# A recommendation tower on one core: the scaled fields go to SBUF, PSUM banks are handed out one at a time, and each tile's sum is taken in two longer reduces

## The reference

```python
e = stack([tbl_f[ids[:, f]] for f in range(39)], axis=1)      # [1024, 39, 16]
x0 = xk = e
for W in (f0, f1, f2):                                        # [39*39,128], [128*39,128], [128*39,128]
    z = einsum('bfd,bgd->bfgd', x0, xk).reshape(b, f * g, d)
    cur = einsum('bpd,pm->bmd', z, W); outs.append(cur); xk = cur
z = sum(concatenate(outs, axis=1), axis=-1)                   # [1024, 384]
h = relu(concat([z, dense_ctx]) @ W_top1 + b_top1)
h = relu(h @ W_top2 + b_top2)
y = h @ W_top3                                                # [1024, 1]
```

## Time and profile before

| | |
|---|---|
| median of 3 runs | 1430.03 us (1429.89 to 1432.74) |
| profiled execution | 1431.03 us, its span 1429.3 us |
| mean granted TensorE clock | 0.987 of full speed |
| PE busy | 1308.0 us (92%) |
| DVE busy | 1128.8 us (79%) |
| ACT busy | 931.4 us (65%) |
| POOL busy | 661.0 us (46%) |

### The profile page before, as it was taken

The page is one execution under the profiler, slowest core; times in us unless marked ns, Lnnn a source line. Parts: engine busy times, 40 slices in busy tenths (PEclk is TensorE's granted clock), DMA queues, the critical chain, the costliest instruction groups (busy, mean ns, idle before and its releaser), DMA issues.

```text
span 1429.3 us, 21569 instructions
## 1 busy us (share of the span) xinstructions
PE 1308.0 (92%) x6680; PEld 984.6 (69%) x6680; DVE 1128.8 (79%) x2797; ACT 931.4 (65%) x3235; POOL 661.0 (46%) x634
## 2 busy tenths in 40 slices
PE   0399999999999999999999999999999999999998
PEld 0356666767777776777777677777767777776777
DVE  2168888888888888788878888788887888787884
ACT  1147776676666677667767667666766677676664
POOL 7785446554444556444455544445464432222100
PEclk9999999999999999999999999999999999999999
DMA  5171021100311012110211003110121002110000
GB/s 134 37 215 40 13 68 49 48 27 3 97 32 35 26 34 76 41 30 13 68 48 48 26 3 93 29 41 27 26 84 42 29 13 66 46 46 25 1 1 1
DMA packets 51178, 63.60 MB, mean 45 GB/s; under 512 B 13067, under 2 KB 24344, under 8 KB 51019
## 3 DMA queue, kind: packets, MB, share of 16 engines
q1 hardware_dynamic: 34544, 56.08, 12.8%
q0 software_dynamic: 10128, 2.98, 1.9%
q10 hardware_dynamic: 6392, 3.18, 0.9%
HBM read 11.08 MB, written 1.02 MB: 8 GB/s over the span
## 4 chain that ended last, share of the span: by engine, by line
PE 65%; DVE 16%; ACT 10%; issue 5%; POOL 3%; DMA 1%; ACTq 0%; DVEq 0%
PE Y L849 14%; PE Y L851 13%; PE Y L850 13%; PE C L783 13%; ACT Y L543 9%; PE C L806 5%; DVE sum_b L694 4%; POOL rows L398 3%; DVE sum_a L694 3%; DVE sum_a L699 3%; DVE part L694 2%; PE C L799 2%; DVE z L663 1%; PE C L824 1%; DVE Y L716 1%
## 5 line engine op out<-in xcount | busy, mean ns | idle before, releaser
L543 ACT ACTIVATE Y<-Y,x_col 128x128 f32<-128x128 f32 x2944 | 792.9, 361 | 387.7 <-PE Y L851 387.1
L849 PE MATMUL Y<-f_high,cur_high 128*128 128x512 f32 (+1 forms) x1280 | 614.5, 480 | 13.3 <-DVE part L707 9.1
L850 PE MATMUL Y<-f_low,cur_high 128*128 128x512 f32 (+1 forms) x1280 | 501.8, 392 | 0.0
L851 PE MATMUL Y<-f_high,cur_low 128*128 128x512 f32 (+1 forms) x1280 | 501.5, 392 | 0.0
L434 POOL TENSOR_TENSOR pairs<-shifted,base 117x512 f32<-117x512 f32 x186 | 240.6, 1295 | 524.1 <-PE C L783 522.4
L398 POOL DMA_INDIRECT rows<-in_tbl_dram,ids_sb x312 | 306.9, 984 | 77.4 <-issue 65.8
L849 PEld LDWEIGHTS Y<-f_high,cur_high 128*128 128x128 f32 x1280 | 243.5, 190 | 124.2 <-issue 54.9
L850 PEld LDWEIGHTS Y<-f_low,cur_high 128*128 128x128 f32 x1280 | 244.4, 191 | 87.3 <-issue 54.3
L851 PEld LDWEIGHTS Y<-f_high,cur_low 128*128 128x128 f32 x1280 | 242.5, 189 | 51.6
L694 DVE SCALAR_TENSOR_TENSOR sum_b<-Y,x_col,sum_b 128x128 f32<-128x128 f32 x768 | 262.7, 342 | 0.2 <-DVE part L694 0.2
L783 PE MATMUL C<-pairs,f_sum 117*128 117x512 f32 (+1 forms) x448 | 241.6, 623 | 5.7 <-DVE pairs L657 5.7
(11 more groups left out here) (92 smaller groups left out, 823.2 us busy)
## 6 DMA issues: line engine op xcount, KB each, us to landing
shifted<-x_seq SPq DMA_DIRECT2D x157, 234.0 KB
base<-x_seq SPq DMA_DIRECT2D x95, 78.0 KB
rows<-in_tbl_dram,ids_sb POOLq DMA_INDIRECT x312
shifted<-x_seq SPq DMA_DIRECT2D x31, 156.0 KB
G<-in_L_rec_f_dram ACTq DMA_DIRECT2D x3, 832.0 KB, 11.8
w_sb<-in_W_top_dram SPq DMA_DIRECT2D x1, 768.0 KB, 13.5
f_ext<-in_L_rec_f_dram SPq DMA_DIRECT2D x1, 760.5 KB
w_sb<-in_W_top_dram SPq DMA_DIRECT2D x1, 512.0 KB, 5.7
```

The costliest lines, as they stand in the source:

```text
L543: ins = act.activation(where[:, i * M:(i + 1) * M], where[:, i * M:(i + 1) * M], ACT.Copy, scale=x_col[:, t // JT % QG, t % JT, f:f + 1])
L849: pe.matmul(where, ch, wh, start=True, stop=False)
L850: pe.matmul(where, ch, wl, start=False, stop=False)
L851: pe.matmul(where, cl, wh, start=False, stop=True).then_inc(y_filled, 1)
```

## The change

ScalarE no longer scales in place: it writes the scaled blocks to a new SBUF tile `scaled_x` of 27 blocks of 128 values. The chunks it takes are now 0, 2, 4, 5, 7 and 8 (24 blocks), and VectorE's fused ones are 1, 3, 6 and 9 (15 blocks). Blocks 0 to 11 of `scaled_x` are chunks 0, 2 and 4; block 12 is the sum of these, block 13 and 14 are the two running sums, and blocks 15 to 26 are chunks 5, 7 and 8. VectorE takes two reduces in a tile, both out of SBUF with neighbouring values 512 bytes apart: one over blocks 0 to 11 (12 x 128 values) into block 12, and one over blocks 12 to 26 (15 x 128 values) into `cur1`. The two additions and the third reduce are gone. `scaled_x` exists once, so ScalarE's chunk 0 of a tile waits for the first reduce of the tile before and its chunk 5 for the second.

The six banks are given out one at a time. A bank is free as soon as ScalarE has scaled its chunk or the fused instructions have read it (`bank_free`). The `G` products take two single banks.

```diff
-UNITS = CH // 2
-UB = 3
-SCALED_UNITS = (0, 2, 4)
-SCALED = tuple(c for c in range(CH) if c // 2 in SCALED_UNITS)
+BANKS = 6
+FUSED = (1, 3, 6, 9)
+SCALED = tuple(c for c in range(CH) if c not in FUSED)
 NSC = len(SCALED)
-SUM_SLOT = 3
-R0, FUSE2, FUSE3, R1, FUSE6, FUSE7, JOIN, MERGE, R2 = 1, 2, 6, 10, 11, 15, 19, 20, 21
-NST = 21
-FREED = {0: R0, 1: R0, 2: FUSE2 + 3, 3: FUSE3 + 3, 4: R1, 5: R1, 6: FUSE6 + 3, 7: MERGE, 8: R2, 9: R2}
+HALF = 4 * (NSC // 2)
+FIRST_SUM, SUM_A = HALF, HALF + 1
+PLACE = {c: 4 * i + (3 if i >= NSC // 2 else 0) for i, c in enumerate(SCALED)}
+PLACES = 4 * NSC + 3
+FUSE = {1: 1, 3: 5, 6: 9, 9: 14}
+R0, R1 = 13, 17
+NST = 17
...
-        sum_a = sb("sum_a", [P, 2, M])
-        sum_b = sb("sum_b", [P, 2, M])
-        part = sb("part", [P, 2, M])
+        scaled_x = sb("scaled_x", [P, PLACES, M])
...
             def scale_chunk(t, c):
                 act.wait_ge(y_filled, CH * t + c + 1)
+                if t and c in (SCALED[0], SCALED[NSC // 2]):
+                    act.wait_ge(acc_steps, NST * (t - 1) + (R0 if c == SCALED[0] else R1))
                 where = bank(t, c)
                 for i, f in enumerate(CH_F[c]):
-                    ins = act.activation(where[:, i * M:(i + 1) * M], where[:, i * M:(i + 1) * M], ACT.Copy,
+                    ins = act.activation(scaled_x[:, PLACE[c] + i, :], where[:, i * M:(i + 1) * M], ACT.Copy,
                                          scale=x_col[:, t // JT % QG, t % JT, f:f + 1])
                 ins.then_inc(scaled, 1)
...
             def tile(t, g, q, j):
                 n0 = NST * t
-                dve.wait_ge(scaled, NSC * t + 2)
-                dve.tensor_reduce(sum_a[:, t % 2, :], unit(t, 0), AX.X, ALU.add).then_inc(acc_steps, 1)
-                fuse(t, 2, FUSE2, 0)
-                fuse(t, 3, FUSE3, 0)
+                fuse(t, FUSED[0])
+                fuse(t, FUSED[1])
                 if j == 0 and q and g >= QG:
                     layer2_read(g // QG - 1, q - 1)
                 if j == JT - 1 and g + 1 < NG:
                     split_cur0(g + 1)
-                dve.wait_ge(scaled, NSC * t + 4)
-                dve.tensor_reduce(part[:, t % 2, :], unit(t, 2), AX.X, ALU.add).then_inc(acc_steps, 1)
-                fuse(t, 6, FUSE6, 1)
-                fuse(t, 7, FUSE7, 1)
...
+                fuse(t, FUSED[2])
+                dve.wait_ge(scaled, NSC * t + NSC // 2)
+                dve.tensor_reduce(scaled_x[:, FIRST_SUM, :], scaled_x[:, 0:HALF, :].rearrange("p s m -> p m s"),
+                                  AX.X, ALU.add).then_inc(acc_steps, 1)
+                fuse(t, FUSED[3])
+                dve.wait_ge(scaled, NSC * t + NSC)
+                dve.wait_ge(acc_steps, n0 + R1 - 1)
                 if j == 0 and g >= 2:
                     dve.wait_ge(s_filled, S_USE["G", g - 2] + 1)
-                dve.tensor_reduce(cur1[:, t % CUR1_RING, :], unit(t, 4), AX.X, ALU.add).then_inc(acc_steps, 1)
+                dve.tensor_reduce(cur1[:, t % CUR1_RING, :], scaled_x[:, FIRST_SUM:PLACES, :].rearrange("p s m -> p m s"),
+                                  AX.X, ALU.add).then_inc(acc_steps, 1)
...
+            def bank_free(use):
+                previous = BANK_PREVIOUS.get(use)
+                if previous and previous[0] == "G":
+                    _, n, r = previous
+                    pe.wait_ge(g_read, 2 * n + r - 1)
+                elif previous:
+                    _, t, c = previous
+                    if c in FUSED:
+                        pe.wait_ge(acc_steps, NST * t + FUSE[c] + len(CH_F[c]) - 1)
+                    else:
+                        pe.wait_ge(scaled, NSC * t + SCALED.index(c) + 1)
```

## The result

The changed kernel takes 1559.93 us (median of 4 runs, 1558.06 to 1560.57), against 1429.96 for the kernel before in the same comparison: a ratio of 1.0915, 95% interval 1.0874 to 1.0955. The forecast was 1559 us. Its profiled execution took 1559.51 us, the span is 1557.8 us.

A forecast was written before the change was run, and what follows sets the result against it. VectorE was to replace TensorE as the bound, its SBUF reduces costing 1.81 ns a value: 84.0 + 44.2 + 1368 (thirty groups at 45.6) + 44.4 + 18.5 = 1559 us, 9% above now. The range was 1450 to 1685 us.

The forecast's parts named there:

- VectorE becomes the bound: Per group: VectorE would need 44.2 us where the kernel takes 41.5, replacing TensorE as the bound.
- 1.81 ns a value: SBUF reduces: rate for values 512 bytes apart, taken from line 636's copy of 624 values, against 1.04 in PSUM.
- The lower bound of 1.63: SBUF reduces: ns a value if a fixed part of 212 ns holds for line 636; total 1493 us, 1450 without stall.
- rival 2: SBUF reduces at half rate by VectorE's own clock, 2.08 ns a value, reduces 3.26 and 4.06 us; 1674 us, chance 0.17.
- A tile at 10.7 us: VectorE's work a tile: fused instructions 3.9, first reduce 2.85, second 3.55, waits for results 0.40 us.
- The stall of 1.4 us in tile 1: VectorE waits for chunk 6 in 31 groups, while TensorE does chunk 5, a first-layer sum and chunk 6 after chunk 1's bank frees.
- The total: Whole kernel: 84.0, group 0 at 44.2, thirty groups at 45.6, the last at 44.4, 16.8 and 1.7; 1559 us.
- Rival 1: SBUF reduces at full rate, 1.04 ns a value, TensorE stays the bound and banks free earlier; 1378 us, chance 0.19.
- about 43 us at the `G` products and 10 at the chunks: TensorE's waits for VectorE that the banks' earlier release would remove if the reduces ran at full rate.
- The turning point: Reduce rate at which VectorE's group, stall included, is 41.5 us, as the kernel now takes: about 1.5 ns a value.
- Rival 3: SBUF reduces wait for GpSimd, 0.3 us each, 256 of them 77 us on top of the forecast; 1636 us, chance 0.05.
- The new waits of ScalarE: Chunks 0 and 5 wait for VectorE's reduces, leaving ScalarE half a tile ahead of need; `C` wanted at slot 13 only.

The follow-up runs named there:

- e1: Changed kernel with both reduces reading neighbouring values of the same SBUF blocks instead of values 512 bytes apart; 1351.64 us, ratio 0.9428 to the kernel before.
- e5: Changed kernel with one first-layer sum of each group moved from ahead of chunk 6 of tile 1 to ahead of chunk 7; 1532.95 us, ratio 1.0711.
- e2: Changed kernel with only the first reduce (line 697) reading neighbouring values; 1448.78 us, ratio 1.0094 to the kernel before.
- e3: Changed kernel whose reduces read by turns in twelve patterns of steps and neighbours, each on its own line; first reduce 1745 ns or 2881 to 3078 ns.
- e4: Changed kernel with 28 blocks stored in interleaved pairs, writes 8 bytes apart, both running sums in the first reduce; 1353.76 us, ratio 0.944 to the kernel before.
- e6: Changed kernel with blocks stored in interleaved fours, writes 16 bytes apart, reduces of 12 and 16 blocks; 1400.05 us, ratio 0.9781 to the kernel before.

## Why the prediction was right, point by point

*VectorE becomes the bound.* Right, and for the reason given: e1 takes the distance away and nothing else, and 208 us go. One sign did not come as written: VectorE's busy share was to be 93% or more, and the page has 89%. The page counts the 86 us before the first fused instruction, too; from there to the last result VectorE is busy for 1367.5 of 1451.9 us, 94%.

*1.81 ns a value, from the copy of line 636.* Measured are (2866 - 154)/1536 = 1.77 and (3579 - 154)/1920 = 1.78. The copy of line 636, one instruction, while two other engines read the same tile, gave the rate within 3%. The lower bound of 1.63 and the two-cycle rate of 2.08 (rival 2, 3.35 us for line 697) are excluded.

*A tile at 10.7 us.* It is 10.6.

*The stall of 1.4 us in tile 1.* 1.58; e5 confirmed its cause: 27 us between the medians, 29 by the two ratios, for 31 x 0.86 = 27. It was 0.2 short because chunk 5, the sum and chunk 6 take 2.53 us on TensorE (731.24 to 733.77) and not 2.36.

*The total.* Groups come at 45.4 us in place of 45.6: from the first to the last result of line 704, 94.67 to 1534.82 us, are 127 tiles of 11.34. The first fused instruction came at 86.33, 2.3 us later than the 84.0 worked out from the kernel before, and the end after the last result's reduce took 19.6 us and not 16.8. These errors cancel: that 1559.0 met 1559.9 is luck in the last few microseconds, not in the mechanism.

```profile
86.33 0.61 DVE L679 TENSOR_SCALAR scaled_x<-Y,x_col 128x128 f32<-128x128 f32 x2 [1.23 <-PE Y L841]
...
94.67 3.60 DVE L704 TENSOR_REDUCE cur<-scaled_x 128x128 f32<-128x1920 f32 x1
...
1534.82 3.37 DVE L704 TENSOR_REDUCE cur<-scaled_x 128x128 f32<-128x1920 f32 x1 [0.63 <-ACT scaled_x L536]
```

*Rival 1, the full rate.* Its condition did not come true, but e1 made it true by force, and its price was wrong: 1378 us, measured 1351.6 (83 us below the kernel before, not 53). The step that failed is "about 43 us at the `G` products and 10 at the chunks". The `G` products gave 1.31 us a group (41 us); the rest was 1.35 us a group (42 us) and not 10, because I took it from the waits view, which counts only the time in which TensorE's modelled rows leave a gap. At the group's end the next start comes 0.49 us later than in e1 (0.67 less 0.18), and that view has 0.33 of it. The turning point was off too: put at 1.5 ns a value, it lies below 1.45, the mean rate of e2's two reduces ((1744 + 3585 - 308) / 3456), with which the time is still 0.9% above the kernel before.

*Rival 3, the lock with GpSimd.* Out: the reduces of line 697 lie between 2790 and 2935 ns in all 128 cases. A wait behind a piece of 1.3 us would have shown.

*The new waits of ScalarE.* They are there, 231 us for the two reduces, and VectorE hardly waits for ScalarE in turn (1.1 us on line 704), as said. But TensorE does. The prediction had `C` wanted "at slot 13 only" and free by then; ScalarE's reading of `G` out of it comes later than that 21 times, 25.8 us in all. On TensorE, in the tile shown above:

```profile
725.70 0.40 PE L841 MATMUL Y<-f_high,cur_low 128*128 128x512 f32 x1
727.41 1.13 PE L767 MATMUL C<-pairs,f_sum 117*128 117x512 f32 x2 [1.31 <-ACT G L519]
```

It costs no time as long as VectorE is the bound: VectorE's stall of 1.58 us follows this wait of 1.31, and in the group where TensorE waits 0.13 us (at 455.6) the stall is 1.57 as well.

## What to carry to other kernels

Before a reduce is moved from PSUM to SBUF, look at how far apart its neighbouring reads will lie: in SBUF steps of 16 bytes and more cost VectorE 1.8 ns a value where 1.04 is the rate; in PSUM, at 512 bytes, they did not. If the data is written by an engine anyway, write it in interleaved pairs; 8 bytes apart cost neither the writer nor the reader any time here. And price a released buffer by the starts of the waiting engine's instructions, stretch by stretch against what that stretch needs, and not by the idle time before them, which for overlapping matmuls showed 0.33 of 0.49 us lost, and of shorter waits next to nothing.

## What the runs showed of the hardware

The step from near to far is sharp: 1744 ns for 1536 values at 8 bytes, 2927 at 16 (e3). At 32 bytes it is a little worse (3078) than at 16, 128 or 512 (2927, 2897, 2881), which I can't explain.

Writes have the same step. On VectorE an instruction that reads its 128 values from PSUM and writes them to SBUF takes 343 ns at 8 bytes (e4) and 435 at 16 (e6), and the fused ones then start 0.35 us apart and not 0.26. On ScalarE the instruction grows from 389 to 487 ns, but the starts stay 0.26 us apart. That is for 128 values; the writes of 320 values pay 1.72 ns a value.

ScalarE's instruction into SBUF at neighbouring addresses is 17 ns longer than into PSUM (378 against 361 ns), which delayed nothing here.
